# A routed expert kernel: the last two token blocks are dispatched pick by pick, and row loads follow the picks

## What is computed

```python
# x (4,256,256), side (4,256,256), cond (4,64); two layers in a row:
x = x + attn(cond(x, side, side, w, u, cond_512), Wq, Wk, Wv, Wg, Wd, Wo)
x = x + ffn(cond2(x, side, side, w2, u2, cond_512), gate_weight, gate_up_weights, down_weights)

def ffn(h):                                   # T = 1024 tokens of 256, 64 experts, 8 picks a token
    logits = h @ gate_weight.T
    probs = softmax(logits)
    routing_weights, selected_experts = lax.top_k(probs, 8)
    routing_weights = routing_weights / routing_weights.sum(-1, keepdims=True)
    combine = zeros((T, 64)).at[arange(T)[:, None], selected_experts].add(routing_weights)
    for wgu, wd, we in (gate_up_weights, down_weights, combine.T):   # per expert
        gate, up = split(h @ wgu, 2, axis=-1)                        # 96 and 96 columns
        acc = acc + we[:, None] * ((silu(gate) * up) @ wd)
    return acc
```

## Time and profile before

| | |
|---|---|
| median of 3 runs | 608.87 us |
| the 3 runs | 609.6, 601.83, 608.87 us |
| the profiled execution, its own time | 608.03 us |
| its span in the trace | 606.2 us |
| TensorE matmul busy | 501.0 us (83%) |
| VectorE, ScalarE, GpSimd busy | 371.4, 331.9, 243.0 us |
| tile loop, first to last tile | 388.1 to about 571 us |
| results fetched and added | about 576 to 606 us |

### The profile page before, as it was taken

How to read it: one execution, slowest core, us unless ns; L and a number is a source line. 1 busy time by engine, 2 the same in 40 slices (tenths; PEclk the granted TensorE clock), 3 DMA queues, 4 the chain that set the end, 5 groups by cost and what they waited for, 6 DMA issues and landing times.

```text
span 606.2 us, 10483 instructions
## 1 busy us (share of the span) xinstructions
PE 501.0 (83%) x2835; PEld 417.9 (69%) x2835; DVE 371.4 (61%) x1194; ACT 331.9 (55%) x982; POOL 243.0 (40%) x255
## 2 busy tenths in 40 slices
PE   1875689798997998998887961399999999999656
PEld 0445568687776786786776551389989998998544
DVE  5657855567547768657778554166666666666334
ACT  3352675585873786866686751055555555555400
POOL 1143301012002245011345567266666766766700
PEclk9895998898997999999988875599999999999869
DMA  8910493200011011110119222599999999995087
GB/s 294 379 54 1 147 334 107 64 2 0 1 55 17 23 51 70 52 20 1 36 48 370 96 82 97 166 340 392 396 384 385 374 385 383 370 384 176 3 345 278
DMA packets 65064, 108.54 MB, mean 179 GB/s; under 512 B 10266, under 2 KB 41191, under 8 KB 64496
## 3 DMA queue, kind: packets, MB, share of 16 engines
q1 hardware_dynamic: 54688, 86.73, 40.7%
q0 software_dynamic: 9168, 16.95, 7.6%
q10 hardware_dynamic: 1152, 4.19, 1.7%
HBM read 81.31 MB, written 34.77 MB: 191 GB/s over the span
## 4 chain that ended last, share of the span: by engine, by line
PE 60%; DVE 19%; ACT 7%; DMA 5%; issue 5%; POOL 3%; ACTq 1%; POOLq 0%; SPq 0%; DVEq 0%
PE ps L1242 14%; PE ps L1027 9%; PE ps L1254 9%; DVE lg L818 4%; PE ps L1143 4%; PE ps L1023 4%; DMA pairs<-pair_rows 4%; PE ps L1024 3%; PE ps L1025 3%; DVE df L750 3%; ACT lg L511 3%; POOL slot_rows L438 2%; PE ps L1072 2%; PE ps L1126 2%; PE ps L1133 2%
## 5 line engine op out<-in xcount | busy, mean ns | idle before, releaser
L497 POOL DMA_INDIRECT pair_rows<-eout,dest x127 | 124.9, 984 | 66.0 <-DVE dest L999 58.4
L1242 PE MATMUL ps<-wts,xg 128*128 128x192 f32 x508 | 104.4, 329 | 0.2 <-DVE xg L998 0.2
L438 POOL DMA_INDIRECT slot_rows<-rows,pair_slot x64 | 64.8, 1012 | 54.9 <-DVE hit L883 37.6
L1242 PEld LDWEIGHTS ps<-wts,xg 128*128 128x128 f32 x508 | 80.1, 192 | 0.7 <-issue 0.6
L682 ACT ACTIVATE sact<-ps 128x96 f32<-128x96 f32 x127 | 31.8, 250 | 85.7 <-PE ps L1242 85.7
L998 DVE COPY xg<-ps 128x256 f32<-128x256 f32 x127 | 53.9, 425 | 36.9 <-PE ps L1027 35.3
L1254 PE MATMUL ps<-wts,aT 96*128 96x256 f32 x254 | 75.9, 380 | 0.0
L564 ACT ACTIVATE lg<-lg,mneg 128x128 f32<-128x128 f32 (+1 forms) x128 | 56.3, 442 | 26.8 <-DVE mneg L818 26.8
L1005 DVE SCALAR_TENSOR_TENSOR aact<-sact,xrow,ps 128x96 f32<-128x96 f32 x127 | 39.9, 314 | 50.1 <-ACT sact L682 50.1
L1027 PE MATMUL ps<-ident,xrow 128*128 128x128 f32 x254 | 49.3, 276 | 16.5 <-DMA xrow<-slot_rows 16.5
L1143 PE MATMUL ps<-oT,wo_sb 128*128 128x256 f32 x256 | 58.1, 380 | 1.4 <-ACT oT L511 1.4
(11 more groups left out here) (189 smaller groups left out, 1145.6 us busy)
## 6 DMA issues: line engine op xcount, KB each, us to landing
wts<-in_experts_dram SPq DMA_DIRECT2D x127, 320.0 KB, 6.7
xrow<-slot_rows SPq DMA_DIRECT2D x127, 130.0 KB, 6.2
slot_rows<-zero SPq DMA_DIRECT2D x1, 8320.0 KB, 29.5
pairs<-pair_rows SPq DMA_DIRECT2D x8, 512.0 KB, 13.4
pairs<-pair_rows ACTq DMA_DIRECT2D x8, 512.0 KB, 13.7
wT<-in_wq_t_dram SPq DMA_DIRECT2D x1, 2048.0 KB, 9.3
wq_raw<-in_wq_l_dram SPq DMA_DIRECT2D x1, 2048.0 KB, 17.8
wo_sb<-in_wo_l_dram SPq DMA_DIRECT2D x1, 2048.0 KB, 17.6
```

The lines of the kernel that those rows point to most:

```text
L438: nc.gpsimd.indirect_dma_start(out=slot_d, out_offset=bass.IndirectOffsetOnAxis(ap=pair_slot[:, t, k:k + 1], axis=0), in_=r[:, k, :], in_o ...
L497: nc.gpsimd.indirect_dma_start(out=pair_d, out_offset=bass.IndirectOffsetOnAxis(ap=dest[:, t:t + 1], axis=0), in_=eout[t % NOUT][:], in_of ...
L1242: ins = nc.tensor.matmul(ps[:, 2 + u % 2, 0:I2], xg[u % 3][:, cc, :], wts[u % NBUF][:, cc * I2:(cc + 1) * I2], start=(cc == 0), stop=(cc = ...
```

## The change

Blocks 6 and 7 are no longer sent one after the other. For each j from 0 to 7, GpSimd sends pick 7-j of block 6 and then pick 7-j of block 7, and the two count on a semaphore `last_sent[j]`. VectorE writes the weights in the same order. The j-th lowest expert of a token can't be below j, so all rows of expert t, for t up to 7, are in `slot_rows` once j has reached t: SyncE waits for `last_sent[t]` ahead of the row load of tile t, and ahead of the first one for the sends of blocks 0 to 5. The ids (column C+1 of `rows`) of both blocks are written before the first send. VectorE's table for tiles 64 to 126 is cut in six steps, of which five stand in tile steps 1 to 5 and the last in step 8, and the two turns of `t_cols` on TensorE move into step 8; a semaphore `cols_read` guards the two PSUM banks that they share with the loop. The loads of `pair_rows` at the end count on the weight tiles' semaphores in place of 16 of their own, on SyncE, ScalarE, VectorE and TensorE alike (shown below for SyncE and VectorE).

```diff
@@ -251,6 +251,8 @@
         pos_done, rows_w, counted, cols_ready, cols_turned, rows_ready = (
             sem(n) for n in ("pos_done", "rows_w", "counted", "cols_ready", "cols_turned", "rows_ready"))
         sent = [sem("sent0"), sem("sent1")]
+        last_sent = [sem(f"last_sent{j}") for j in range(TOPK)]
+        cols_read = sem("cols_read")
         key_made = sem("key_made")
         wts_ld = [sem(f"wts_ld{i}") for i in range(NBUF)]
         rows_ld = [sem(f"rows_ld{i}") for i in range(NBUF)]
...
@@ -299,6 +300,9 @@
 
         turn_bank = lambda t: 4 if t in (NTB - 3, NTB - 1) else 3
         sent_ahead = lambda t: 16 * TOPK * (t // 2)
+        LAST = (NTB - 2, NTB - 1)
+        pair_landing = lambda b, h: 16 * (len(range(2 * b + h, TILES, NBUF)) + 1)
+        COLS_AT = 8
 
         block = ctx.enter_context(nc.Block())
 
...
@@ -363,10 +367,12 @@
             for t in range(NBUF):
                 load_wts(t, slice(t, t + 1))
             for i in range(2):
-                sp.wait_ge(sent[i], 16 * TOPK * (NTB // 2))
+                sp.wait_ge(sent[i], sent_ahead(LAST[i]))
             for t in range(NE):
                 if t >= NBUF:
                     load_wts(t, slice(t, t + 1))
+                if t < TOPK:
+                    sp.wait_ge(last_sent[t], 16 * len(LAST))
                 load_rows(t, slice(t * CAP, t * CAP + P))
             sp.wait_ge(rows_ready, 1)
             for t in range(NE, TILES):
...
@@ -382,7 +388,7 @@
                 sp.wait_ge(scattered[i], 16 * len(range(i, TILES, NOUT)))
             for b in range(0, NTB, 2):
                 for h in range(2):
-                    sp.dma_start(pairs[b][:, h * HK:(h + 1) * HK], pair_block(b, h)).then_inc(pairs_ld[b][h], 16)
+                    sp.dma_start(pairs[b][:, h * HK:(h + 1) * HK], pair_block(b, h)).then_inc(wts_ld[2 * b + h], 16)
             for b in range(NTB):
                 if b % 2:
                     sp.wait_ge(y_copied, b // 2 + 1)
...
@@ -487,8 +493,19 @@
             nc.gpsimd.iota(i_off[:], pattern=[[P, NMORE]], base=P, channel_multiplier=0, allow_small_or_imprecise_dtypes=True)
             nc.gpsimd.iota(ei_row[:], pattern=[[CAP, NE], [P, NMORE]], base=0, channel_multiplier=0,
                            allow_small_or_imprecise_dtypes=True).then_inc(consts_ready, 1)
-            for t in range(NTB - 2, NTB):
-                send_rows(t)
+            for t in LAST:
+                pool.wait_ge(sent[t % 2], sent_ahead(t))
+                nc.gpsimd.iota(rows[t % 2][:, :, C + 1], pattern=[[1, TOPK]], base=t * P * TOPK, channel_multiplier=TOPK,
+                               allow_small_or_imprecise_dtypes=True).then_inc(ids_set, 1)
+            pool.wait_ge(ids_set, NTB)
+            for j in range(TOPK):
+                k = TOPK - 1 - j
+                for i, t in enumerate(LAST):
+                    pool.wait_ge(rows_x, t + 1)
+                    pool.wait_ge(rows_w, TOPK * LAST[0] + 2 * j + i + 1)
+                    nc.gpsimd.indirect_dma_start(
+                        out=slot_d, out_offset=bass.IndirectOffsetOnAxis(ap=pair_slot[:, t, k:k + 1], axis=0),
+                        in_=rows[t % 2][:, k, :], in_offset=None).then_inc(last_sent[j], 16)
             for t in range(TILES):
                 pool.wait_ge(out_copied, t + 1)
                 pool.wait_ge(dest_ready, t + 1)
...
@@ -963,31 +980,48 @@
             route_pick(NB - 1)
             route_key(NB - 1)
             route_slots(NB - 1)
-            route_rows(NTB - 2)
-            route_rows(NTB - 1)
+            dve.wait_ge(rows_w, TOPK * LAST[0])
+            for t in LAST:
+                dve.wait_ge(sent[t % 2], sent_ahead(t))
+            for j in range(TOPK):
+                k = TOPK - 1 - j
+                for i, n in enumerate(LAST):
+                    m = 2 * j + i
+                    if m >= TOPK:
+                        dve.wait_ge(rows_w, TOPK * LAST[0] + m - TOPK + 1)
+                    V.scalar_tensor_tensor(out=hit[:, m % TOPK, :], in0=key[:, n % TB, :], scalar=ktop[:, n, k:k + 1], in1=rcomb[:, n % TB, :],
+                                           op0=ALU.is_equal, op1=ALU.mult, accum_out=rows[n % 2][:, k, C:C + 1]).then_inc(rows_w, 1)
             dve.wait_ge(consts_ready, 2)
             dve.wait_ge(counted, 1)
             cnt = ps[:, 0, 0:NE]
             flat = lambda a: a.rearrange("p e i -> p (e i)")
             link(V.tensor_scalar(valid[:, 0:NE], cnt, iota_p[:, 0:1], None, ALU.is_gt))
             link(V.tensor_scalar(to_dump[:, 0:NE], valid[:, 0:NE], 1.0, dump_p[:, 0:1], ALU.is_lt, ALU.mult))
-            link(V.tensor_tensor(t_left[:], cnt.unsqueeze(2).to_broadcast([P, NE, NMORE]),
-                                 i_off[:].unsqueeze(1).to_broadcast([P, NE, NMORE]), ALU.subtract))
-            V.tensor_scalar(t_num[:], t_left[:], float(P), None, ALU.min)
-            link(V.tensor_scalar(t_has[:], t_left[:], 0.0, None, ALU.is_gt))
-            V.tensor_tensor_scan(out=flat(t_ord[:]), data0=ones[:, 0:1].to_broadcast([P, NE * NMORE]), data1=flat(t_has[:]),
-                                 initial=0.0, op0=ALU.mult, op1=ALU.add)
-            link(V.tensor_tensor(t_row[:], t_num[:], ei_row[:], ALU.add))
-            link(V.tensor_tensor(t_ord[:], t_ord[:], t_has[:], ALU.mult))
-            for k, of in enumerate((t_row, t_num)):
-                ins = V.scalar_tensor_tensor(out=flat(t_one[:]), in0=flat(t_ord[:]), scalar=tile_no[:, 0:1], in1=flat(of[:]),
-                                             op0=ALU.is_equal, op1=ALU.mult, accum_out=t_cols[:, k:k + 1])
-                link(ins)
-            V.tensor_copy(t_one[:, 0, 0:1], t_cols[:, 0:1]).then_inc(cols_ready, 1)
-            dve.wait_ge(cols_turned, 1)
-            V.tensor_copy(t_rows[:], ps[:, 5, 0:P]).then_inc(rows_ready, 1)
-            link(V.tensor_scalar(valid[:, NE:TILES], ps[:, 5, P:P + MORE], iota_r[:, 0:1], None, ALU.is_gt))
-            link(V.tensor_scalar(to_dump[:, NE:TILES], valid[:, NE:TILES], 1.0, dump_p[:, 0:1], ALU.is_lt, ALU.mult))
+            V.tensor_tensor(t_left[:], cnt.unsqueeze(2).to_broadcast([P, NE, NMORE]),
+                            i_off[:].unsqueeze(1).to_broadcast([P, NE, NMORE]), ALU.subtract).then_inc(cols_read, 1)
+            dve.wait_ge(cols_read, 1)
+
+            def tile_table(step):
+                if step == 0:
+                    V.tensor_scalar(t_num[:], t_left[:], float(P), None, ALU.min)
+                    link(V.tensor_scalar(t_has[:], t_left[:], 0.0, None, ALU.is_gt))
+                elif step == 1:
+                    V.tensor_tensor_scan(out=flat(t_ord[:]), data0=ones[:, 0:1].to_broadcast([P, NE * NMORE]), data1=flat(t_has[:]),
+                                         initial=0.0, op0=ALU.mult, op1=ALU.add)
+                    link(V.tensor_tensor(t_row[:], t_num[:], ei_row[:], ALU.add))
+                elif step == 2:
+                    link(V.tensor_tensor(t_ord[:], t_ord[:], t_has[:], ALU.mult))
+                elif step < 5:
+                    of = (t_row, t_num)[step - 3]
+                    link(V.scalar_tensor_tensor(out=flat(t_one[:]), in0=flat(t_ord[:]), scalar=tile_no[:, 0:1], in1=flat(of[:]),
+                                                op0=ALU.is_equal, op1=ALU.mult, accum_out=t_cols[:, step - 3:step - 2]))
+                    if step == 4:
+                        V.tensor_copy(t_one[:, 0, 0:1], t_cols[:, 0:1]).then_inc(cols_ready, 1)
+                else:
+                    dve.wait_ge(cols_turned, 1)
+                    V.tensor_copy(t_rows[:], ps[:, 5, 0:P]).then_inc(rows_ready, 1)
+                    link(V.tensor_scalar(valid[:, NE:TILES], ps[:, 5, P:P + MORE], iota_r[:, 0:1], None, ALU.is_gt))
+                    V.tensor_scalar(to_dump[:, NE:TILES], valid[:, NE:TILES], 1.0, dump_p[:, 0:1], ALU.is_lt, ALU.mult).then_inc(cols_read, 1)
 
             for s in range(TILES + 1):
                 u = s - 1
...
@@ -996,8 +1030,14 @@
                     if s >= 3:
                         dve.wait_ge(gu_done, s - 2)
                     V.tensor_copy(xg[s % 3][:], ps[:, s % 2, 0:C].rearrange("p (a t) -> p a t", a=CC)).then_inc(xt_copied, 1)
+                    if s == NE:
+                        dve.wait_ge(cols_read, 2)
                     V.scalar_tensor_tensor(out=dest[:, s:s + 1], in0=xrow[s % NBUF][:, C + 1:C + 2], scalar=valid[:, s:s + 1],
                                            in1=to_dump[:, s:s + 1], op0=ALU.mult, op1=ALU.add).then_inc(dest_ready, 1)
+                    if s == COLS_AT:
+                        tile_table(5)
+                    elif 1 <= s < 6:
+                        tile_table(s - 1)
                 if u >= 0:
                     dve.wait_ge(silu_done, u + 1)
                     if u >= 2:
...
@@ -1008,7 +1048,7 @@
             for b in range(0, NTB, 2):
                 y = pairs[b]
                 for h in range(2):
-                    dve.wait_ge(pairs_ld[b][h], 16)
```

(14 more changed lines are left out.)

5 lines of the change are left out of this document (2 added, 3 removed).

## The result

| | before | after |
|---|---|---|
| median | 607.74 us (4 runs, 601.83 to 609.6) | 596.91 us (4 runs, 594.87 to 597.51) |
| the profiled execution, its own time | 608.03 us | 594.87 us |
| its span | 606.2 us | 593.1 us |
| mean granted clock of TensorE | 0.918 | 0.934 |

The ratio is 0.984, with an interval of 0.980 to 0.987: the kernel takes 10.8 us less. The forecast was 599.5 us, 593 to 604, with 8.7 us gained.

What follows compares the result with a forecast made beforehand. Bound: TensorE's tile loop, started late by GpSimd's 16 sends and their landing. Gain 9.0 us at tile 7 less 0.3 for the table's turns, 8.7 us, gives 599.5 us median; range 593 to 604, the forecast's own 597 to 602.

Steps and rivals of the forecast that it cites:

- Tile 7 as the landmark: Start of tile loop: tile 7, not tile 0, waits for all 16 sends; its turn moves from 397.73 to 388.7, gaining 9.0 us.
- Tiles 0 to 6 done by then: Tile loop: tile 0's rows land at 369.7, a pair every 2.7 us; even at half clock the tiles end before 388.
- The second send waits for the copy of block 7: GpSimd's sends: second send starts at 364.16 + 0.80 = 364.96 instead of 364.45, costing 0.5 us.
- 14 sends in 14 x 1.343 - 0.15 = 18.65 us: GpSimd's other 14 sends: before's mean spacing 1.343 us, less 0.15 for an id write now ahead, ending at 383.6.
- 983 instead of 960 ns beside VectorE: GpSimd's sends beside VectorE's work: 983 ns as in line 497, against 960 for line 438; 14 x 0.023 = 0.3 us.
- Landing 2.52 + 2.24 us: After the last send: 2.52 us to the row load and 2.24 us to TensorE, giving 388.4.
- more than forecast: Rival: no slow send and no cost beside VectorE, gain 9.9 us, 598.3 us; 18% for below 596.7.
- Clock at tile 7: TensorE at tile 7: full clock assumed; half would lose about 1.5 us, gain 7.2, time 601; 10% for that rival.
- The table's other steps at 0: VectorE's table steps 0 to 4 cost 0, in steps with over 1 us of slack; last step 0, at most 0.8.
- Weights and SyncE at 0: Tile 16's weight loads start at 390.4, need about 6.7 us, are asked for at 402.9; slack 5.8 us, cost 0.
- sends slowed by VectorE: Rival: each table step costs a send 0.8 us, gain 5.4, time 602.5; 7% for 602 to 604, 3% for slower than before.
- loads eat it: Rival: transfers set the loop after tile 16, so TensorE would only wait for weights; 606 to 609 us, 6%.

Runs made afterwards that it cites:

- four_early: Changed kernel with only tiles 0 to 3 loaded behind their picks, the load of tile 4 waiting for all the rest; 602.70 us, ratio 0.994.
- experiments 1 to 4: Changed kernel with no load behind a pick (606.68 us), half of them (602.70), a GpSimd fill before the last pair (598.25), eight more VectorE copies (595.96).
- after_2: The changed kernel itself, unedited, timed again on the second chip beside the kernel before; 644.13 us, 12 runs, ratio 0.992.
- Experiment 5: Changed kernel with five more VectorE additions of 448 columns, both inputs in SBUF, while VectorE waits for tile 0; 643.13 us, one run, second chip.
- experiment 4: Changed kernel with eight more VectorE copies of 448 float32 columns, SBUF to SBUF, while VectorE waits for tile 0; 595.96 us, one run.
- experiments 6 and 7: Changed kernel with the last table step and turns in tile step 6 (643.61 us, 0.991), or the whole table ahead of the loop (643.97 us, 0.990); second chip.

## Why the prediction was right, point by point

- **Tile 7 as the landmark: right, and shown.** First send to tile 7's turn fell from 34.57 to 24.23 us. `late_loads`, which undoes the row loads behind picks alone, gives all of it back (34.78 us, ratio 1.000), `four_early` 6.1 of the 10.3 us.
- **Tiles 0 to 6 done by then: right on the first chip, not on the second.** In after the turn of tile 7 waits 0.92 us for its rows, so TensorE was ready. In the eight traces of the second chip it doesn't wait, and comes 3 to 5 us later than in after.
- **The second send waits for the copy of block 7: wrong by 0.5 us.** It starts 1.29 us after the first, as before. The copy ends at 360.48 and the send starts at 360.77: 0.3 us behind the release, not 0.8, and no more than the ordinary gap between sends. The 0.8 holds where GpSimd has been at rest before the wait; here it came from the send just before.
- **14 sends in 14 x 1.343 - 0.15 = 18.65 us: 0.9 us too much.** They took 378.48 - 360.77 = 17.71 us, 1.265 each. The mean of before held a send of 1.78 us that I left in (0.8 us of the 0.9), and a second one of 1.12 us at 370.33 that I overlooked. Whether a slow one occurs hangs on where the scan falls between the sends: none in after, but one of 1.58 to 1.82 us in seven of the twelve other traces of the changed kernel and its versions, so these 0.8 us are luck.
- **983 instead of 960 ns beside VectorE: 0.3 us that were not there.** Line 506 has a median of 961 ns. The 983 of line 497 belong to that send's own kind, not to what runs beside it.
- **Landing 2.52 + 2.24 us: 0.5 too little.** 3.02 to the load and 2.21 from there to TensorE (378.48, 381.50, 383.71). In the other five traces of before and experiments 1 to 4 the sum is 4.5 to 4.9 us, so this is scatter. On the second chip it can't be read so, since TensorE is late there.
- **Sum of these:** 8.7 + 0.5 + 0.9 + 0.3 - 0.5 = 9.9 us, and the trace gives 10.3 - 0.35 = 10.0. The difference of the medians is 10.8. So the term that was sized wrong is the pace of the sends; what the rival "more than forecast" named (no slow send, no cost beside VectorE, 598.3 us) is what happened, and the last 0.8 us of the medians are within their spread. Against the 19 runs of before beside experiments 1 to 4 (606.47 us) the difference would be 9.6 us, if the first measurement ran on that chip, which isn't on record.
- **Clock at tile 7: right.** In after it is 1.00 from 378 on, through the stretch 380 to 382 where TensorE works 0.85 of 2 us. Up to 376 it was at 0.50: the sparse stretch did run slow, as half of that paragraph feared, but behind the denser one (4.00 us of work in the 4 us from 374 on) it was up in time. In `after_2`, on the second chip, it was at 0.50 until 400 us, just ahead of tile 7.
- **The two turns in step 8: right.** The step of tile 8 takes 386.81 - 385.18 = 1.63 us and that of tile 9 1.51, against 1.42: 0.3 us.
- **The table's other steps at 0: right here, but the cover was named too generally.** `late_loads` prices them without the waits for rows at about 0.8 us, the step of 2.17 us in place of 1.41.
- **Weights and SyncE at 0: right here.** TensorE works 16.00 of 16 and 100.00 of 100 us, though a weight tile now lands 9.2 us after issue instead of 6.7. The nine row loads ahead of tile 16's weights took 385.75 - 381.50 = 4.25 us on SyncE, as costed (9 x 0.47).
- **The rival "sends slowed by VectorE": it does occur, at the price of up to 0.86 us for one send, but not in after.** Experiment 5 shows it for instructions with two inputs in SBUF (sends of 1.33 and 1.30 us), and experiment 4 for `t_num` with one (1.13 us). Whether copies hold a send, experiment 4 can't say, since none of its sends starts in the middle of one.
- **The rival "loads eat it": not on the first chip, and open on the second.** There the ratio is 0.992 instead of 0.984, about 5 us. One part of what is missing is that tile 7's turn comes 29.3 us after the first send instead of 24.2 (experiments 6 and 7). The other may be the loop behind it. In `after_2`, TensorE is busy 43.72 of the 50 us from 450 on at the full clock, and 308 GB/s are moved:

```profile
450.00:500.00 50.00, 43.72 (x263) 37.01 (x262) 23.95 (x87) 21.80 (x86) 28.55 (x29) 1.00 0.95 308
```

  Against 50.00 of 50 in the earlier trace rows. A loop that isn't bound by TensorE can give less for an earlier start; without a trace of before on this chip the two parts can't be told apart. Why it isn't bound by TensorE, no run here shows: the rests end with waits of many kinds.

## What to carry to other kernels

When a stage waits for all of a scattered transfer, order the transfer by what its first reader needs and let the readers follow piece by piece; the gain is the work that fits before the last piece, and here the clock was up by then too: 1.00 from 378 us on in after, where `four_early`, with a rest of 6.68 us before tile 4, had 0.50 at 384 to 386. Check on the trace that this work is in fact done when the last piece lands: on the second chip it wasn't, and the gain there is about half. Price a wait by what the waiting engine did just before (0.3 us after a send, 0.8 us from rest here), and keep a single slow instruction out of a mean. Before moving work "between" the steps of a loop, ask what would show it if the cover were gone.
